# Edge softmax of a graph layer: attention and message columns interleaved in threes of wider products, with the last numerators on GpSimd

## The reference

```python
h = jnp.maximum(_layernorm(x, axis=-1), 0.0)
w_m = (efeat @ W_msg + b_msg).reshape(E, in_f, -1)
w_a = (efeat @ W_attn + b_attn).reshape(E, in_f, -1)
h_src = feat[src][:, :, None]
e1 = w_m * h_src
e2 = w_a * h_src
seg_max = jax.ops.segment_max(e2, dst, num_segments=N)
ex = jnp.exp(e2 - seg_max[dst])
denom = jax.ops.segment_sum(ex, dst, num_segments=N)
attn = ex / denom[dst]
ft = jax.ops.segment_sum(e1 * attn, dst, num_segments=N)
x = x + ft.sum(axis=1)
```

## Time and profile before

| | |
|---|---|
| Median of the three runs | 9786.86 us (9780.59, 9786.86, 9788.02) |
| Span of the profiled execution, first to last instruction | 9780.2 us |
| What lies around that span | 0.4 us to the run of 9780.59, the nearest of the three |
| Busy: PE, DVE, POOL, ACT | 7946.4, 7357.8, 7256.3, 3060.5 us |
| The softmax stage, 4000 to 6000 us: PE, DVE, ACT, POOL busy | 1568.4, 1968.3, 1539.3, 1514.8 us |
| DMA in the same stretch | share 0.71, 202 GB/s |

### The profile page before, as it was taken

The page is one execution under the profiler, slowest core; times in us unless marked ns, Lnnn a source line. Parts: engine busy times, 40 slices in busy tenths (PEclk is TensorE's granted clock), DMA queues, the critical chain, the costliest instruction groups (busy, mean ns, idle before and its releaser), DMA issues.

```text
span 9780.2 us, 134112 instructions
## 1 busy us (share of the span) xinstructions
PE 7946.4 (81%) x37269; PEld 4276.1 (44%) x37269; DVE 7357.8 (75%) x13651; ACT 3060.5 (31%) x12664; POOL 7256.3 (74%) x5177
## 2 busy tenths in 40 slices
PE   0899996999984777777777777745999995899994
PEld 0466663555541333333333333323655554555552
DVE  2566663454545999999999999987888885688884
ACT  0111111000004777777777777742000000000000
POOL 5677775777767777777777777745888887688887
PEclk6999996999997999999999999977999997899997
DMA  1333332222213777777777777766222221333331
GB/s 32 101 101 106 104 101 52 67 60 68 68 46 91 202 201 200 202 205 201 200 201 203 203 202 200 201 186 190 70 82 69 82 69 47 99 106 99 99 104 48
DMA packets 490722, 1215.28 MB, mean 124 GB/s; under 512 B 236141, under 2 KB 273304, under 8 KB 469836
## 3 DMA queue, kind: packets, MB, share of 16 engines
q1 hardware_dynamic: 242522, 996.22, 31.8%
q0 software_dynamic: 212624, 110.62, 9.1%
q10 hardware_dynamic: 35440, 106.85, 3.3%
HBM read 419.84 MB, written 787.23 MB: 123 GB/s over the span
## 4 chain that ended last, share of the span: by engine, by line
PE 27%; POOL 26%; issue 23%; DVE 19%; DMA 2%; DVEq 1%; SPq 1%; ACT 0%; POOLq 0%; ACTq 0%
POOL arena L559 26%; PE PS L949 21%; DVE arena L1687 5%; DVE arena L1691 4%; PE PS L971 4%; DVE arena L1733 3%; DVE arena L1700 2%; DVE arena L1711 2%; PE PS L932 1%; DVEq L1679 1%; DVE arena L1813 1%; DMA arena<-d_lane 0%; DVE tmp L1815 0%; DVE arena L1422 0%; DVE arena L1721 0%
## 5 line engine op out<-in xcount | busy, mean ns | idle before, releaser
L949 PE MATMUL PS<-arena,TB 125*128 125x500 bf16 (+1 forms) x18711 | 4067.9, 373 | 109.2 <-DVE arena L1390 109.1
L559 POOL DMA_INDIRECT arena<-d_feat,srci x1650 | 2578.1, 1562 | 842.0 <-issue 454.2
L949 PEld LDWEIGHTS PS<-arena,TB 125*128 125x128 bf16 x18711 | 1832.9, 99 | 2013.2 <-issue 174.7
L559 POOL DMA_INDIRECT arena<-d_h,srci x1485 | 1887.5, 1271 | 653.0 <-issue 433.1
L770 ACT ACTIVATE arena<-PS,arena 125x32 f32<-125x32 f32 x10560 | 2012.4, 446 | 302.8 <-PE PS L1068 263.0
L1390 DVE TENSOR_SCALAR arena<-arena,lane 125x2000 bf16<-125x2000 f16 (+2 forms) x1848 | 1228.9, 723 | 348.0 <-PE PS L949 221.9
L1402 DVE SCALAR_TENSOR_TENSOR arena<-arena,lane,PS 128x500 f32<-128x500 f16 x891 | 637.1, 715 | 1120.9 <-PE PS L949 858.5
L559 POOL DMA_INDIRECT arena<-d_rel,irel x858 | 1210.2, 1411 | 307.2 <-issue 261.2
L559 POOL DMA_INDIRECT arena<-d_nn,srci x759 | 1068.6, 1408 | 283.4 <-issue 230.4
L1115 PE MATMUL PS<-arena,ident 125*125 125x512 f32 x1650 | 873.6, 610 | 403.6 <-ACT arena L813 210.1
L1733 DVE SCALAR_TENSOR_TENSOR arena<-arena 125x512 f32<-125x512 f32 x1155 | 859.7, 744 | 20.3
(11 more groups left out here) (274 smaller groups left out, 7172.5 us busy)
## 6 DMA issues: line engine op xcount, KB each, us to landing
d_soft_max<-arena SPq DMA_DIRECT2D x165, 1120.0 KB
d_soft_den<-arena SPq DMA_DIRECT2D x330, 560.0 KB
d_soft_num<-arena SPq DMA_DIRECT2D x330, 560.0 KB
arena<-d_pick SPq DMA_DIRECT2D x66, 843.8 KB
arena<-d_lane SPq DMA_DIRECT2D x66, 843.8 KB
d_x<-arena ACTq DMA_DIRECT2D x165, 241.7 KB
arena<-d_x SPq DMA_DIRECT2D x165, 241.7 KB
d_rel<-arena SPq DMA_DIRECT2D x50, 669.4 KB
```

What stands on the lines that cost most here:

```text
L559: gp.indirect_dma_start(out=dst, out_offset=None, in_=table, in_offset=bass.IndirectOffsetOnAxis(ap=index, axis=0)).then_inc(S(sem), 16)
L949: ins = pe.matmul(PS[:, acc_at(L, q):acc_at(L, q) + w], TB[:, part, g * LANES * F:(g + 1) * LANES * F], OH[L][i][:, g, at:at + w], start=g ...
```

## The change

The two kinds of columns are interleaved. `XM` holds the maxima alone, and `XD[slot, step, 512]` the pairs: 16 columns of attention, then the 16 of the message for the same input feature, and so on; `paired(rows, a)` picks one kind out of it, as runs of 16 with a step of 32. `W6` is loaded in the same order. So a group's product is one instruction of 1024 elements that reads and writes in one piece, three a block in place of six. The numerators of a block, five instructions of two steps before, become three on DVE, of two, four and two steps (`weigh(0, 2)`, `weigh(2, 4)`, `weigh(6, 2)`), and one on POOL for the last two steps (`late_numerators`), which stands in POOL's list behind the ten gathers of the block three further on. DVE waits for it (`soft_late`) ahead of its last sum.

Stores: the maxima go to memory as before. The sums go by columns 0 to 255 and 256 to 511 of each step (`d_sums`), which lie 256 values at a time in SBUF, five such runs a partition and store, where one run of 1280 values went before.

Behind the last block, DVE copies three rows into `CB` for the transposes, and the loop over the nodes reads its rows by pairs.

```diff
+            def late_numerators(b):
+
+                s = b % 3
+                gp.wait_ge(S("soft_exp"), 6 * b + 1)
+                rows = XD[:, s, B1 - 2:B1, :]
+                gp.tensor_tensor(paired(rows, 1), paired(PB[:, s, NA - 2:NA], 1), paired(rows, 0), ALU.mult)                    .then_inc(S("soft_late"), 1)
+
             gp.wait_ge(S("tab_soft"), 16 * NT)
             for b in range(NB1):
                 s = b % 3
...
                 for t in range(B1):
                     gather(GH[:, s, t, :], d_feat, srci[:, b * B1 + t:b * B1 + t + 1], f"soft_g{s}")
+                if b >= 3:
+                    late_numerators(b - 3)
...
-            def product(b, s, g, a):
+            def product(b, s, g):
 
                 n, t, at = GROUPS[g], 2 * g, 2 * (g % 2) * 512
-                if a == 0:
-                    dve.wait_ge(S("soft_mm"), NG3 * b + g + 1)
-                v.tensor_tensor(XS[:, s, 1 + a, t:t + n, :].rearrange("p t (i o) -> p t i o", i=F),
-                                PS[0:P, at:at + n * 512].rearrange("p (t a i o) -> p t a i o", a=2, i=F, o=F)[:, :, a],
-                                GH[:, s, t:t + n, :].unsqueeze(3).broadcast_to([P, n, F, F]),
-                                ALU.mult).then_inc(S("soft_prod" if a else "soft_at"), 1)
+                dve.wait_ge(S("soft_mm"), NG3 * b + g + 1)
+                v.tensor_tensor(XD[:, s, t:t + n, :].rearrange("p t (i c) -> p (t i) c", i=F),
+                                PS[0:P, at:at + n * 512].rearrange("p (x c) -> p x c", c=2 * F),
+                                bc(GH[:, s, t:t + n, :].rearrange("p t i -> p (t i)"), 2 * F),
+                                ALU.mult).then_inc(S("soft_prod"), 1)
...
-                def weigh(t):
+                def weigh(t, n):
 
                     dve.wait_ge(S("soft_exp"), 6 * b + (B1 - t) // 2)
-                    rows = XS[:, s, 2, t:t + 2, :] if t < AT else PB[:, s, t - AT:t - AT + 2, 1, :]
-                    v.tensor_tensor(XS[:, s, 2, t:t + 2, :], rows,
-                                    XS[:, s, 1, t:t + 2, :], ALU.mult).then_inc(S("soft_num"), 1)
...
+                    rows = XD[:, s, t:t + n, :] if t < AT else PB[:, s, t - AT:t - AT + n, :]
+                    sums = XD[:, s, t:t + n, :]
+                    v.tensor_tensor(paired(sums, 1), paired(rows, 1), paired(sums, 0), ALU.mult).then_inc(S("soft_num"), 1)
...
+                        if t in (2, AT):
+                            dve.wait_ge(S("soft_num"), 3 * b + (2 if t == 2 else 3))
+                        if t == B1 - 2:
+                            dve.wait_ge(S("soft_late"), b + 1)
                         dve.wait_ge(S("soft_sum"), (B1 - 2) * b + t - 1)
                     ins = v.scalar_tensor_tensor(to, last, KR[:, s, t, 1:2], to, ALU.mult, ALU.add)
                     ins.then_inc(S("soft_sum"), 1)
                     yield
-                    if t % 2:
-                        weigh(t + 1)
+                    if t == 1:
+                        weigh(2, AT - 2)
+                        yield
+                    if t == 3:
+                        weigh(AT, NA - 2)
                         yield
...
-            def put(b, s, a, t, n):
-                wide_dma(sp, edges_w(d_soft[a])[:, bass.ds(b * (B1 * CH) + t * CH, n * CH)],
-                         XS[:, s, a, t:t + n, :].rearrange("p t c -> p (t c)"), f"soft_s{s}")
+            def put_sums(b, s, t, n):
+                for a, table in enumerate(d_sums):
+                    wide_dma(sp, edges_w(table)[:, bass.ds(b * (B1 * CH) + t * CH, n * CH)].rearrange("p (t c) -> p t c", t=n),
+                             XD[:, s, t:t + n, a * CH:(a + 1) * CH], f"soft_s{s}")
```

More of the change, by code:

```diff
@@ L262, in graph_layers, with paired @@
         assert PB_END <= o <= AR, o
+        def paired(rows, a):
+            if len(rows.shape) == 3:
+                rows = rows.rearrange("p t c -> p (t c)")
+            return rows.rearrange("p (x a o) -> p x a o", a=2, o=F)[:, :, a, :]
         NODE = ar(0, 2 * 5 * ROW).rearrange("p (s j c) -> p s j c", s=2, j=5)
@@ L306, in graph_layers @@
         d_w = dram("d_w", [F, R, F])
-        d_soft = [dram(f"d_soft_{a}", [E, CH]) for a in ("max", "den", "num")]
+        d_smax = dram("d_smax", [E, CH])
+        d_sums = [dram(f"d_sums_{a}", [E, CH]) for a in ("low", "high")]
         d_rel = dram("d_rel", [N * R, TW])
@@ L1761, in soft @@
                 next(new)
-                product(b, s, 2, 1)
                 next(new)
```

142 lines of the change are left out of this document (76 added, 66 removed).

## The result

The changed kernel takes 9859.1 us (median of five runs, 9813.9 to 9897.1) beside 9787.5 us for the kernel before on the same chip. The ratio of the two is 1.0072, interval 1.0058 to 1.0085: slower by 0.7%, where 9721 was forecast and 9850 was the top of the range.

A forecast was written before the change was run, and what follows sets the result against it. DVE was taken to set the 20.72 us beat, POOL to become the bound at 20.3: 0.42 x 164 = 69 us less, 3 more behind the blocks, 66 in all, giving 9721 us, range 9655 to 9850.

The forecast's parts named there:

- the port: Rival at SBUF: DVE's two-SBUF-input instructions stand still during POOL's multiplication, up to 1.25 us a block, 9873 us; chance 0.18.
- DVE's own sum: Softmax stage, DVE: products -0.20, numerators -0.88, maxima +0.34, together -0.74 us a block, beat 19.98 if DVE alone sets it.
- The last of the signs named: DVE would wait if three maxima between carry and first sum leave PE too little time for the carry's matmuls; no size.
- POOL's term: POOL's list per block: 15.71 + 11 x 0.305 + M = 19.06 + M, taken as a beat of 20.3 us.
- M: Time of POOL's new multiplication of 512 elements: between 0.88 and 1.65 us, taken as 1.25.
- The named bound: POOL was to become the softmax stage's bound at 20.3 us a block, 0.3 above DVE; chance 0.42.
- POOL's wait for the product: POOL's wait once a block for DVE's product, 2.28 us, was to go.
- The stretch of the gathers: Rival: stores in shorter runs stretch POOL's gathers, beat 20.77 (9798 us) or 22.1 (10016 us); chance 0.15.
- The sign named for this rival: In the changed kernel's profile, a gathers' mean over 1.62 us would point to the stores.
- Paired runs: DVE's runs of 16 with a step of 32, costed at nothing; as rival 1.2 us lost, beat 21.18, 9865; chance 0.05.
- The signs given for the port: Mean of DVE's maximum above 478 ns or sums above 744, or POOL's multiplication far above 1.65 us.

The follow-up runs named there:

- late_rows: The changed kernel with the sums stored in runs of 1280 values, as before, at other places in memory: 9861.8 us, 1.0095 of the kernel before.
- b_spare: The kernel before plus a POOL multiplication of 512 spare elements, awaited by nobody, behind each ten gathers: 10091.5 us, 1.0308.
- a_dve: The changed kernel without POOL's multiplication, DVE weighing the last two steps too: 9939.7 us, 1.0146 of the kernel before.
- a_rows: a_dve with the sums stored in runs of 1280 values, as before, at other places in memory: 9823.3 us, 1.0039 of the kernel before.
- b_order_small: b_order with each store of the sums sending one step of five, the node loop reading the maxima instead: 9898.0 us, 1.0115.
- b_order: The kernel before with numerators between DVE's maxima and the third group's second product 3 us earlier: 9963.0 us, 1.0174.
- a_spare: a_dve plus a POOL multiplication of 512 spare elements, awaited by nobody, behind each ten gathers: 10082.7 us, 1.0296.
- after_sync: The changed kernel with two one-element DVE memsets and POOL's multiplication behind the seventh gather, waiting for DVE's last sum: 9749.7 us, 0.9965.
- a_write: a_dve plus a POOL memset of 1536 spare elements, which reads nothing, behind each ten gathers: 10034.9 us, 1.0249.

## Why the prediction was wrong

- **The step that failed** is "the port": the multiplication would meet the third product, "so most of it should meet that one, and only its rest the maxima behind". On that ground the sum put the loss on DVE at nothing. The multiplication meets the maxima: 1.05 us of it beside them and 0.28 beside the product. It was to start 3.7 us into the block and started anywhere from 0.6 to 5.9, since the gathers ahead of it took 1.21 to 6 us; and DVE can lose more than the time of the multiplication, 1.63 us for 1.30 in the block shown above. 1.09 us a block were paid, more than the 0.74 named as the point from which this rival decides. The rival itself was right in mechanism and place. That its beat of 21.23 is 0.03 from the measured one, and its 9873 14 us from the time, is partly luck: it took 1.25 for the loss, and an own term of 0.13 was missing. Its chance of 0.18 was too low for a case that rested on the place of an instruction on POOL that nothing ties to DVE's block.
- **DVE's own sum**, -0.74, came out at -0.61: products 1.21 as forecast, numerators 1.22 and 0.68. What I left out is that the first maximum now waits for its own product, which stands right ahead of it (start to start 1.26 in place of 1.13). 20.72 - 0.61 + 1.09 = 21.20, the beat as measured; 0.48 x 164 + 3 = 82 us, against 77 in the spans (9857.2 and 9780.2). The last of the signs named, a wait for PE's carry, is there but small: 10.9 us in 94 blocks.
- **POOL's term.** M was chosen as 1.25 and is 1.30. Its sum is 10 x 1.636 + 2.89 + 1.32 = 20.6 where 20.3 stood, below DVE's 21.20. The named bound was the wrong one. That POOL's wait for the product would go was nearly right (0.72 a block of 2.28 left), for another reason.
- **The stretch of the gathers** was put down to the stores ("The 3.6 us of stretch lie where the stores run"). They lie where DVE runs sums and maxima. A coincidence in one timeline was read as a cause. The sign named for this rival did show, gathers above 1.62 us (1.636), and misled: late_rows has 1.642 with the long runs of before and is as slow as the changed kernel. So the rival (0.15) has no part in the result.
- **Paired runs** at no cost: right (686 and 1219 ns for the numerators).
- The signs given for the port were the ones that showed: the mean of a maximum above 478.

The Trainium skill's rule that was named as this rival (SBUF — State Buffer, "Who interferes with whom") held: two SBUF inputs on VectorE against a GpSimd instruction that reads, 682 to 1028 ns in b_spare, and none for one that only writes. It has the instruction that starts first keep the port and the loser wait for the other's length. By the records of b_spare it was otherwise: the numerator started first and lost, and it lost 1.9 us to 1.26.

**Open.** Within a run of sums and maxima some gathers get in at the next boundary, most only at the end of the run; which of the two is not explained, nor are the 436 that got in within an instruction. Nor is it why short runs cost some 105 us in a_dve (a_rows) and nothing in the changed kernel. What the gather needs at its start wasn't tried; that it is a read of its indices is a guess.

## What to carry to other kernels

Before work is given to GpSimd, look at what VectorE does at that moment: here it was free beside an instruction that reads PSUM, and beside one with two SBUF inputs it could cost more than its own duration. Tie it to such a place with a semaphore, since one that floats ends up where the queue ahead of it leaves it. And a VectorE order without a gap can hold up GpSimd's gathers: taking the harmful multiplication away made the kernel slower (1.0072 to 1.0146), and two one-element memsets a block, 59 ns each, in the run brought it to 0.9977.

## What the runs showed of the hardware

- A gather of 1.21 us took up to 7.5 us in an unbroken run of DVE sums and maxima with two SBUF inputs, at 100 GB/s of DMA (b_order_small) as at 192 (b_order), and ended 1.16 us after the product behind the run began.
- In the middle of a DVE instruction that reads PSUM 3316 gathers got what they need at their start, in the middle of a numerator, with two SBUF inputs, 3.
- DVE lost 1.7 to 1.8 us a block to a POOL multiplication of 1.27 us (b_spare, a_spare), and nothing to one of 1.29 us that lay beside a product of 1.21 us (after_sync), nor to a POOL memset of 1.40 us (a_write).
- Two maxima of which the second needs the first start 0.52 us apart; with another instruction behind it a maximum takes 0.39. A maximum that reads the wide product right ahead of it starts 1.26 us behind it, any other 1.13.
